# Scaled keys and values: twelve ScalarE copies a chunk become three GpSimd broadcast multiplications

## What is computed

```python
def step(carry, inp):
    w0_, w1_, w2_ = carry
    qi, ki, vi, lr0i, lr1i, lr2i = inp
    gate = ki @ w0_
    hb = ki @ w2_
    sg = silu(gate)
    hidden = sg * hb
    dhidden = vi @ w1_.transpose(0, 2, 1)
    dhbm = dhidden * sg
    dgate = dhidden * hb
    dgba = silu_backprop(dgate, gate)
    w1g = newtonschulz5(jnp.einsum('bch,bcd->bhd', hidden * lr1i, vi))
    w0g = newtonschulz5(jnp.einsum('bcd,bch->bdh', ki * lr0i, dgba))
    w2g = newtonschulz5(jnp.einsum('bcd,bch->bdh', ki * lr2i, dhbm))
    ...
    oi = silu(qi @ w0_) * (qi @ w2_) @ w1_
    return ((w0_, w1_, w2_), oi)
```

## Time and profile before

| | |
|---|---|
| median of 3 runs | 909.52 us (907.36 to 911.2) |
| span of the profiled execution, first to last instruction | 904.6 us |
| own time of the profiled execution | not listed apart from the runs; the median run lies 4.9 us above the span |
| PE | busy 832.8 us, 92% |
| DVE | busy 687.1 us, 76% |
| ACT | busy 649.7 us, 72% |
| POOL | busy 348.1 us, 38% |

### The profile page before, as it was taken

The page is one execution under the profiler, slowest core; times in us unless marked ns, Lnnn a source line. Parts: engine busy times, 40 slices in busy tenths (PEclk is TensorE's granted clock), DMA queues, the critical chain, the costliest instruction groups (busy, mean ns, idle before and its releaser), DMA issues.

```text
span 904.6 us, 16298 instructions
## 1 busy us (share of the span) xinstructions
PE 832.8 (92%) x4972; PEld 512.3 (57%) x4972; DVE 687.1 (76%) x2354; ACT 649.7 (72%) x1417; POOL 348.1 (38%) x285
## 2 busy tenths in 40 slices
PE   6999999999999999999999999998799987999993
PEld 3657667575766757576575756656454433444441
DVE  3898989889898988989898898988795524544441
ACT  3878888888888988888888898887674313444430
POOL 2333444454444445344444534443142331222222
PEclk9999999999999999999999999999799999999997
DMA  9955517153351624425162440458424564545550
GB/s 328 331 155 174 150 62 197 45 181 104 109 154 63 206 60 152 118 94 142 58 177 65 124 118 24 130 189 255 105 47 86 88 126 64 83 82 87 86 82 5
DMA packets 79126, 111.01 MB, mean 123 GB/s; under 512 B 14128, under 2 KB 35760, under 8 KB 78400
## 3 DMA queue, kind: packets, MB, share of 16 engines
q1 hardware_dynamic: 70720, 92.85, 36.0%
q0 software_dynamic: 8176, 16.85, 9.6%
q10 hardware_dynamic: 144, 0.26, 0.1%
HBM read 47.22 MB, written 64.55 MB: 124 GB/s over the span
## 4 chain that ended last, share of the span: by engine, by line
PE 63%; DVE 15%; ACT 8%; DMA 6%; issue 4%; POOL 3%; SPq 0%; DVEq 0%; POOLq 0%; ACTq 0%
PE bank L128 17%; PE bank L134 8%; PE bank L1090 7%; PE bank L1104 3%; DMA out_x<-t_arena,t_tokx 3%; POOL t_small L2930 2%; PE bank L609 2%; PE bank L705 2%; DVE t_small L1583 2%; ACT t_arena L2528 1%; PE bank L646 1%; PE bank L614 1%; PE bank L632 1%; PE bank L641 1%; PE bank L684 1%
## 5 line engine op out<-in xcount | busy, mean ns | idle before, releaser
L128 PEld LDWEIGHTS bank<-t_arena 128*128 128x128 bf16 (+1 forms) x1536 | 123.1, 122 | 111.2 <-issue 30.3
L128 PE MATMUL bank<-t_arena 128*128 128x128 bf16 (+1 forms) x1536 | 155.9, 236 | 12.9 <-ACT t_arena L2537 6.4
L1090 PE MATMUL bank<-t_arena 128*128 x200 | 91.8, 602 | 3.6 <-ACT t_arena L2856 3.6
L3081 POOL DMA_INDIRECT out_x<-t_arena,t_tokx x25 | 38.5, 1539 | 106.8 <-DMA out_x<-t_arena,t_tokx 74.8
L134 PE MATMUL bank<-t_ident,t_arena 128*128 128x128 f32 x398 | 65.9, 281 | 14.5 <-DVE t_arena L1139 6.1
L134 PEld LDWEIGHTS bank<-t_ident,t_arena 128*128 128x128 f32 x398 | 45.9, 142 | 49.8 <-issue 17.6
L2856 ACT ACTIVATE t_arena<-t_arena,t_small 128x128 f32<-128x128 f32 x100 | 41.1, 482 | 39.8 <-DVE t_tokx L2233 39.6
L2936 POOL TENSOR_TENSOR t_small<-t_small,t_half 128x8 f32<-128x8 f32 x14 | 24.5, 1747 | 103.5 <-DVE t_small L1583 103.5
L1090 PEld LDWEIGHTS bank<-t_arena 128*128 128x128 f32 x200 | 36.7, 193 | 41.2 <-issue 41.2
L128 PE MATMUL bank<-t_W,t_arena 128*128 128x128 f32 x384 | 53.8, 284 | 0.6 <-ACT t_W L2436 0.2
L128 PEld LDWEIGHTS bank<-t_W,t_arena 128*128 128x128 f32 x384 | 47.8, 195 | 4.3 <-issue 4.1
(11 more groups left out here) (1118 smaller groups left out, 2383.3 us busy)
## 6 DMA issues: line engine op xcount, KB each, us to landing
xs_scratch<-t_arena SPq DMA_DIRECT2D x16, 2064.0 KB, 11.9
t_arena<-xs_scratch SPq DMA_DIRECT2D x156, 64.0 KB, 1.9
t_arena<-in_gate_up SPq DMA_DIRECT2D x32, 256.0 KB, 3.7
wm_scratch<-t_arena SPq DMA_DIRECT2D x30, 256.0 KB
t_arena<-in_wmod SPq DMA_DIRECT2D x5, 1024.0 KB, 10.4
t_arena<-in_down SPq DMA_DIRECT2D x16, 256.0 KB, 3.1
out_x<-t_arena SPq DMA_DIRECT2D x16, 256.0 KB, 2.0
t_arena<-wm_scratch SPq DMA_DIRECT2D x4, 1024.0 KB, 4.9
```

What stands on the lines that cost most here:

```text
L128: mm = pe.matmul(bank[:, s], lhs[:, s], rhs[:, s], start=True, stop=True)
L1090: mm = pe.matmul(AA(u)[:, :], xT[u % 2][:, 128 * k:128 * k + 128], w_e[:, bass.ds(which[u], 1), 512 * k:512 * k + 512], start=(k == 0), st ...
L3081: pool.indirect_dma_start(out=out, out_offset=bass.IndirectOffsetOnAxis(ap=tokx[b % RING], axis=0), in_=xg[b % RING], in_offset=None, boun ...
```

## The change

In chunks 1 to 15, `kl2`, `kl0` and `vl` are made on GpSimd, each by one multiplication of a whole 128x512 tile by learning rates that are repeated along 128 columns. The twelve scaled copies of 128x128 on ScalarE go. Chunk 0 keeps its copies on ScalarE, under a semaphore of its own. The readers and the writers of these tiles wait for the semaphore `kl_pool` in place of `prep_act`. The instruction orders of PE and DVE stay as they were.

```diff
-PREP_ACT = ("hT", "raw0", "raw1", "sq", "raw2", "vT", "kT", "qT", "kl2", "kl0", "vl")
+PREP_ACT = ("hT", "raw0", "raw1", "sq", "raw2", "vT", "kT", "qT")
+KL_ACT = ("kl2", "kl0", "vl")
+KL_POOL = ("kl2", "kl0", "vl")
...
-                pe.wait_ge(prep_act, nth(PREP_ACT, c, "kl2"))
+                pe.wait_ge(kl_pool, nth(KL_POOL, c-1, "kl2"))
...
-                pe.wait_ge(prep_act, nth(PREP_ACT, c, "vl"))
+                pe.wait_ge(kl_pool, nth(KL_POOL, c-1, "vl"))
...
-                dve.wait_ge(prep_act, nth(PREP_ACT, p-2, "kl0"))
-                dve.wait_ge(prep_act, nth(PREP_ACT, p-2, "vl"))
+                if p == 2:
+                    dve.wait_ge(kl_act, nth(KL_ACT, 0, "vl"))
+                if p >= 3:
+                    dve.wait_ge(kl_pool, nth(KL_POOL, p-3, "vl"))
...
-                act.wait_ge(prep_act, nth(PREP_ACT, p-1, "kl0"))
+                act.wait_ge(kl_pool, nth(KL_POOL, p-2, "kl0"))
                 act.activation(raw[1], P1[:, :], ACT.Silu).then_inc(prep_act, 1)
...
-                act.wait_ge(prep_act, nth(PREP_ACT, p-1, "vl"))
+                act.wait_ge(kl_pool, nth(KL_POOL, p-2, "vl"))
                 act.activation(raw[2], P0[:, :], ACT.Silu).then_inc(prep_act, 1)
...
-                act.wait_ge(rate_dve, nth(RATE_DVE, p, "lr"))
-                act.wait_ge(prep_dve, nth(PREP_DVE, p, "tk"))
-                act.wait_ge(n2_pe, nth(N2_PE, p-2, "G"))
-                for h in range(H):
-                    s = slice(128 * h, 128 * h + 128)
-                    row = act.activation(kl2[p % 2][:, s], raw[1][:, s], ACT.Identity, scale=lr12[p % 2][:, 8 + h:9 + h])
-                row.then_inc(prep_act, 1)
...
+            pool.wait_ge(rate_dve, nth(RATE_DVE, 1, "lr"))
+            pool.wait_ge(prep_dve, nth(PREP_DVE, 1, "tk"))
+            pool.tensor_tensor(h4(kl2[1]), h4(raw[1]), bc(lr12[1][:, 8:12]), ALU.mult).then_inc(kl_pool, 1)
+            pool.tensor_tensor(h4(kl0[1]), h4(raw[1]), bc(lr12[1][:, 0:4]), ALU.mult).then_inc(kl_pool, 1)
+            pool.wait_ge(prep_act, nth(PREP_ACT, 1, "raw2"))
+            pool.tensor_tensor(h4(vl[1]), h4(raw[2]), bc(lr12[1][:, 4:8]), ALU.mult).then_inc(kl_pool, 1)
...
+                pool.wait_ge(rate_dve, nth(RATE_DVE, p, "lr"))
+                pool.wait_ge(prep_dve, nth(PREP_DVE, p, "tk"))
+                pool.wait_ge(n2_pe, nth(N2_PE, p-2, "G"))
+                pool.tensor_tensor(h4(kl2[p % 2]), h4(raw[1]), bc(lr12[p % 2][:, 8:12]), ALU.mult).then_inc(kl_pool, 1)
                 pool.wait_ge(apply_dve, nth(APPLY_DVE, a, "dl"))
                 pool.tensor_tensor(ed, euler[:, 0:1], dl, ALU.pow).then_inc(apply_pool, 1)
+                pool.wait_ge(n0_pe, nth(N0_PE, p-2, "G"))
+                pool.tensor_tensor(h4(kl0[p % 2]), h4(raw[1]), bc(lr12[p % 2][:, 0:4]), ALU.mult).then_inc(kl_pool, 1)
+                pool.wait_ge(prep_act, nth(PREP_ACT, p, "raw2"))
+                pool.wait_ge(n1_pe, nth(N1_PE, p-2, "G"))
+                pool.tensor_tensor(h4(vl[p % 2]), h4(raw[2]), bc(lr12[p % 2][:, 4:8]), ALU.mult).then_inc(kl_pool, 1)
```

More of the change, by code:

```diff
@@ L91 @@
 PREP_FIRST_PE = ("T", "m13", "m23", "kT", "vT", "m03", "qT")
-PREP_FIRST_ACT = ("hT", "raw1", "sq", "raw2", "kT", "vT", "kl2", "kl0", "vl", "raw0", "qT")
+PREP_FIRST_ACT = ("hT", "raw1", "sq", "raw2", "kT", "vT", "raw0", "qT")
 FIRST = {PREP_PE: PREP_FIRST_PE, PREP_ACT: PREP_FIRST_ACT}
@@ L303, in adaln_block @@
         prep_act = sem("prep_act")
+        kl_act = sem("kl_act")
+        kl_pool = sem("kl_pool")
         rate_pe = sem("rate_pe")
@@ L418, in _ @@
             pe.matmul(P2[:, :], hT[0][:, 128:256], wqkv[0][:, 1, :], start=False, stop=False)
-            pe.wait_ge(prep_act, nth(PREP_ACT, 0, "kl2"))
+            pe.wait_ge(kl_act, nth(KL_ACT, 0, "kl2"))
             pe.wait_ge(fwd_dve, nth(FWD_DVE, 0, "dhm"))
@@ L429, in _ @@
             pe.wait_ge(fwd_dve, nth(FWD_DVE, 0, "hid"))
-            pe.wait_ge(prep_act, nth(PREP_ACT, 0, "vl"))
+            pe.wait_ge(kl_act, nth(KL_ACT, 0, "vl"))
             pe.wait_ge(fwd_dve, nth(FWD_DVE, 0, "dgt"))
@@ L737, in _ @@
             heads(pe, A0, ap_s, W[1]).then_inc(apply_pe, 1)
-            pe.wait_ge(prep_act, nth(PREP_ACT, NC - 1, "kl2"))
+            pe.wait_ge(kl_pool, nth(KL_POOL, NC - 2, "kl2"))
             pe.wait_ge(fwd_dve, nth(FWD_DVE, NC - 1, "dhm"))
@@ L747, in _ @@
             pe.wait_ge(fwd_dve, nth(FWD_DVE, NC - 1, "hid"))
-            pe.wait_ge(prep_act, nth(PREP_ACT, NC - 1, "vl"))
+            pe.wait_ge(kl_pool, nth(KL_POOL, NC - 2, "vl"))
             pe.wait_ge(fwd_dve, nth(FWD_DVE, NC - 1, "dgt"))
@@ L2301, in _ @@
                 row = act.activation(kl2[0][:, s], raw[1][:, s], ACT.Identity, scale=lr12[0][:, 8 + h:9 + h])
-            row.then_inc(prep_act, 1)
+            row.then_inc(kl_act, 1)
             act.wait_ge(fwd_pe, nth(FWD_PE, 0, "hb"))
@@ L2424, in _ @@
             act.copy(qT[1], P0[:, :]).then_inc(prep_act, 1)
-            act.wait_ge(rate_dve, nth(RATE_DVE, 1, "lr"))
-            act.wait_ge(prep_dve, nth(PREP_DVE, 1, "tk"))
-            for h in range(H):
-                s = slice(128 * h, 128 * h + 128)
[L2429 to L2434, removed]
             act.wait_ge(n0_pe, nth(N0_PE, 0, "TW"))
@@ L2440, in _ @@
             act.copy(W[2][:, :], B2[:, :]).then_inc(n2_act, 1)
[L2441 to L2445, removed]
             for c in range(1, NC - 1):
@@ L2597, in _ @@
                 act.copy(W[1][:, :], B1[:, :]).then_inc(n1_act, 1)
[L2598 to L2603, removed]
             act.wait_ge(apply_pe, nth(APPLY_PE, NC - 2, "gq"))
@@ L3207, in _ @@
             sp.wait_ge(prep_act, len(PREP_ACT) * NC)
+            sp.wait_ge(kl_pool, len(KL_POOL) * (NC - 1))
             sp.wait_ge(prep_dve, len(PREP_DVE) * NC)
```

## The result

The changed kernel takes 942.84 us (median of 4 runs, 941.12 to 945.87), the kernel before 908.44 in the runs beside it (4 runs, 907.22 to 911.2). The ratio is 1.0369, 95% interval 1.0339 to 1.0399: slower, by 34.4 us. The profiled execution took 944.24, with a span of 942.5.

The account below looks back on a forecast made before the run. TensorE bounds the kernel almost without a break, with VectorE just ahead. 14 passes at 2.43 give 34.0 us, plus 1 for chunk 1, minus 3 for slow clock: +32 on the 904.6 span, plus 4.9 to the median, 942 us; range 913 to 968.

Parts of the forecast that it names:

- The likeliest case: GpSimd multiplications and two-input VectorE operations hold each other each pass: 942 us, 925 to 958 over T; chance 0.55.
- T: Length of one 512-column GpSimd multiplication: taken as 1.2 us, between bounds of 0.8 and 1.6.
- `WT[0]` held: After the merge, VectorE's scaling of WT[0] (L1680) waits until kl2's multiplication ends: 1.09 us late, and TensorE's transposes too.
- L1703 and L1708 held: Two-input VectorE operations held until kl0's and vl's multiplications end: 2.04, then 2.92 us late in all.
- −0.36 and −0.13: VectorE's slacks in a pass: 0.36 us that dhm waits for sg, 0.13 that dgb ends ahead of its product.
- `rs` "stays just ahead of `hA`": On GpSimd behind the scatter DMAs, rs is moved by nearly the same as hA, so hA does not wait.
- The slow clock: In three passes TensorE's halved clock behind the merge makes a late VectorE cost less: 1 us each, −3.
- Copies of `W[0]` earlier: "nothing": ScalarE's copies of W[0] come earlier, but TensorE reads W[0] after its transposes: priced at nothing.
- VectorE is never held: Rival: GpSimd alone waits, the DMAs and rs slip, hA 0.7 to 1.4 us late: 920 to 930, say 924; chance 0.13.
- No change: Rival: neither engine holds the other over these tiles, nothing moves: 908 to 911 us; chance 0.11.
- faster: Rival: no holding, and the 0.36 us that dhm waits for sg counts on the chain: 904.5 us; chance 0.04.
- More slow clock: Rival: added TensorE idle time halves its clock in the other 11 passes too, up to 18 us more, 960; chance 0.13.

Follow-up runs that it names:

- run 2: Kernel before, plus three GpSimd memsets of 1024 uint8 columns a pass, which read nothing, at the places of the multiplications: 917.68 us, ratio 1.0094.
- run 3: Kernel before, plus three GpSimd one-input products (one tile times a constant) a pass at the places of the multiplications, results unused: 923.69 us, ratio 1.016.
- run 9: Changed kernel with only kl2 and kl0 on GpSimd, behind posu, vl back on ScalarE, rs before the scatter DMAs, one merge moved behind posu: 907.55 us, ratio 0.9979.
- run 10: Changed kernel with only kl2 and kl0 on GpSimd, behind posu, vl on ScalarE, rs before the scatter DMAs, the merge not moved: 908.32 us, ratio 0.9998.
- run 1: Kernel before with all ScalarE copies kept, plus the three GpSimd multiplications into columns that nobody reads: 944.84 us, ratio 1.0391.
- run 5: Changed kernel with kl2 alone on GpSimd, kl0 and vl again ScalarE copies: 931.83 us, ratio 1.0236.
- run 6: Kernel before, nothing new on GpSimd, plus one unused VectorE reduction of a tile right ahead of the scaling of WT[0]: 932.17 us, ratio 1.0261.
- run 7: Changed kernel with the next pass's rs issued ahead of the two scatter DMAs on GpSimd: 938.37 us, ratio 1.0325.

## Why the prediction held, step by step

The time was 942.84 against 942, by the predicted mechanism. The likeliest case was the right one, but several terms were off and cancelled, and that the two times agree to 1 us is luck: the increase was 34.4 in place of 32, on a kernel before that ran 1.1 faster than the prediction's 909.52.

- **T.** Taken as 1.2, measured 1.04, and 1.00 from start to start. The estimate from the GPSIMD Engine Reference of the Trainium skill (section "Elementwise — side-by-side cycle accounting"), 1.1, was nearer; the trace puts it lower still.
- **`WT[0]` held.** Predicted 1.09 late, measured 0.83. It is not the scaling itself that is held, but L1684 in front of it, which reads a single tile of 4 columns. That a two-input scaling of 512 columns is held too shows in chunk 1 (last section). The page SBUF — State Buffer of the Trainium skill (section "Who interferes with whom") names `tensor_scalar` and casts among the operations that can contend with GpSimd in a two-port mode; runs 2 and 3 and the changed kernel agree, and the one-column `tensor_scalar` L1707 beside it was never held.
- **L1703 and L1708 held.** Predicted 2.04 and 2.92 late in sum; the order was as written, and the holds add to 2.15, since T is shorter. With −0.36 and −0.13 that makes 1.66 of VectorE's lateness at `dgb`'s product, in place of 2.43.
- **`rs` "stays just ahead of `hA`".** This step failed. Before, `rs` ended 0.44 ahead of `hA`, and of this the prediction's own steps left 0.08 (the DMAs 2.92 late, `hA` 2.56). But the second DMA takes 1.29 in place of 0.97 and `rs` 0.83 in place of 0.58, so `rs` is 0.48 late. VectorE runs two-input work beside both, and I read it as in rows 5, GpSimd held by VectorE; no run separates this. It needs no multiplication: in the first pass of the kernel before, the two DMAs take 1.20 and 1.44 and `rs` 0.82, and `hA` waits as long (the row below, of before). With this wait the pass grows by 2.20.

```profile
114.43 0.55 DVE L1471 TENSOR_SCALAR t_arena<-t_arena,t_small 128x512 f32<-128x512 f32 x1 [0.48 <-POOL t_small L2924]
```
- **Sum.** 14 × 2.20 = 31 in place of 34. Chunk 1 was taken as 1 and measured 3.15: there the three run back to back, and each holds an instruction, for 0.85, 0.84 and 0.83. The slow clock was taken as −3: before, two of the thirteen passes have it and cost 1.29 more each; after, five cost 0.13 to 0.29 more, together 1.3, which makes −1.3. Another −0.55 has nothing to do with the clock: it is the wait for `rs` that the first pass of the kernel before had already. The sum is 32 again. The profiled spans differ by 37.9, which is this sum, the 4.1 of the start, and 1.6 in the tail that I have not followed. The third slow pass before, the fourteenth, lies in that tail, and between the profiles whose pass is 38.79 to 39.06 the part behind the last copy of `qT` varies from 289.3 to 293.0 by itself.
- **Copies of `W[0]` earlier: "nothing".** Under-priced: 0.26 a pass where VectorE is not late (runs 9 and 10). In the changed kernel VectorE is late, and nothing of it shows. The 0.14 by which `W[0]` was there ahead of its first product was therefore not all slack.

The rivals: "VectorE is never held" falls with the three held instructions and with runs 1 to 3. "No change" and "faster" fall with the result. "More slow clock" did not happen in the changed kernel: its transposes are 0.83 late as well, yet 8 of 13 passes keep the full clock, and the slow ones cost at most 0.29 more. In four of those five VectorE waits up to 0.88 for the rank product behind the slow transposes, and by then `vl` has ended: L1709 is held 0.12 longer, but L1714 not at all, which gives 0.72 back (0.88 + 0.12 − 0.72 = 0.28). From one of them:

```profile
158.07 0.17 DVE L1702 TENSOR_TENSOR t_small<-bank,t_base 128x8 f32<-128x8 f32 x1 [0.88 <-PE bank L721]
...
159.83 0.16 DVE L1714 TENSOR_TENSOR t_arena<-t_small 128x1 f32<-128x1 f32 x1
```

In runs 5, 6 and 7 it did happen, in nearly all passes. What decides between the changed kernel and run 7, with the same 0.83, was not found: the rows of the two differ ahead of the transposes by nothing that I could name, so this stays open.

## What to carry to other kernels

Before moving work to GpSimd, read in the timeline what VectorE does at that place. The multiplications were harmless under VectorE's work on banks and single tiles of 512 columns, and cost 2.2 us a pass under tiny operations that stood on the path. The length of the operation matters less than the place. A short wait of the busiest engine can cost more than itself: two edits that make it late are not to be added up from single runs, since each may bring the slow clock by itself.

## What was not expected of the hardware

- A GpSimd operation with one input holds VectorE for a part of its length: 0.63 of 1.49 us. The page SBUF — State Buffer of the Trainium skill (section "SBUF: two separate sides") says that whoever starts first has the shared pair for the whole instruction. For the multiplication the trace agrees (1.04 of 1.04), for the one-input operation it does not, and the measurement decides.
- The one-input product with bfloat16 output took 1.49 us, the broadcast product with two inputs 1.04, to bfloat16 as to float32.
- The hold works both ways in turn. In chunk 1 of the changed kernel `WT[0]`'s scaling begins just ahead of `vl`, which becomes 0.52 longer, and the next scaling then takes 0.83 longer and ends 0.54 after `vl`:

```profile
72.02 0.68 DVE L1438 TENSOR_TENSOR t_WT<-t_WT,t_small 128x512 f32<-128x512 f32 x1
72.04 1.56 POOL L2898 TENSOR_TENSOR t_arena<-t_arena,t_small 128x512 f32<-128x512 f32 x1
72.62 1.52 DVE L1440 TENSOR_TENSOR t_WT<-t_WT,t_small 128x512 f32<-128x512 f32 x1
```

- A wait of TensorE of 0.59 us ahead of its transposes was enough to bring a granted clock of 1.2 GHz behind it in every row of run 6, while in most passes of the changed kernel a wait of 0.83 at the same place was not.
